# A wavelet-attention and mixture-of-experts block: the order of expert 0's last products, and expert 14 in one block

## Chip, core and metric

One Trainium2 chip, one core. The metric is device time in microseconds, the median of several runs of one kernel; a profile is one more execution, with its own time.

## What is computed

The input is x, [2, 1024, 128]. A first layer (layer norm, two wavelet levels, linear attention on the lowest band, synthesis, layer norm, residual) gives 2048 tokens of 128 features. The second layer, where the change lies, is a mixture of 16 experts that choose their tokens:

```python
scores = sigmoid(h @ gate_w.T)                       # h: 2048 normalised tokens
cap = 256                                            # 2048 / 16 * 2
topk_score, topk_ids = top_k(scores.T, cap)          # each expert takes 256 tokens
xin = h[topk_ids]
eo = silu(xin @ gw.T + gb) * (xin @ up_w.T + up_b)   # 128 -> 512, per expert
eo = eo @ down_w.T + down_b                          # 512 -> 128
out = zeros.at[topk_ids].add(eo * topk_score)
shared = (silu(x @ sh_gate.T) * (x @ sh_up.T)) @ sh_down.T   # 128 -> 256 -> 128, all tokens
result = x + out + shared
```

All of it is in 32-bit floating point.

## The kernel before, in words

Tokens lie 128 to a partition block: 16 tiles of 128 tokens, in 4 groups of 4. The first layer, the router and the search for each expert's 256th score take the first 95 us or so. Each expert's tokens then come as two chunks of 128 rows, and four engines and the DMA queues work on the experts as a pipeline whose order is written out by hand; waits are semaphores.

- **POOL** issues indirect DMAs. `gather(e, c)` (line 538) fetches chunk c of expert e's rows from DRAM into one of 7 buffers (they lie in the tensor that the profile calls hT). `scatter(e)` (line 549) adds both weighted chunks of expert e into the output, chunk after chunk; it waits first until all scatters of the expert before have landed (for expert 0: until the four base stores have), then for each chunk's weighed rows. 12 gathers go ahead; then, after each scatter, 2 (experts 0 to 5) or 1 (experts 6 to 13) gathers follow, by the tuple `BETWEEN`.
- **TensorE (PE)** takes an expert as a block of 4 products q of 128 hidden features each. `turn_x` (line 1443) transposes the gathered rows; for each q the up and gate products (lines 1488, 1489) write one of five banks; `down(q)` (line 1457) multiplies hidden features back, two products later (`LAG = 2`), into bank 3 or 4 by turns. The turn of the next expert stands in the middle of a block (after its third product).
- **ACT** does silu on each product (line 745) and `weigh`, the scaling of an expert's finished rows by their scores (line 571, one instruction for each chunk), which releases the scatter.
- **DVE** does `hidden` (line 1122), the copy of turned rows out of PSUM (`keep_x`, line 1088), the down bias (`add_bias`, line 1104), and, in the first three experts, pieces of the table that places the last eight experts' rows (lines 1020 to 1030).
- **SP** stores the base, x1 plus the shared part, group by group (line 399); the last group's store waits for `add_shared(LAST, ...)` on DVE (line 1055).

Experts 14 and 15 (`HALVED = E - 2`) are not whole blocks but two half blocks each, one for each chunk, so that a chunk can be scattered while the other is computed:

```python
BLOCKS = [(e, WHOLE) for e in range(HALVED)] + [(e, (c,)) for e in range(HALVED, E) for c in range(CH)]
WARM_B = {HALVED + 1: 2, HALVED + 2: 2, HALVED + 3: 2}
```

A half block's turn stands at its own beginning, behind the last downs of the block before. `WARM_B` puts filler products (line 1145, their result is not used) ahead of the turns of the last three half blocks.

The shared expert's last group (`shared_down(LAST, t)`, line 1343) is computed among expert 0's products, after the second one, into bank 6; expert 0's fourth product, which uses bank 6 again, waits until DVE has added it up. Expert 0's last two downs come after expert 1's first product (q = 4), and ACT weighs expert 0's rows after its silu of that product.

## Time and profile before

| what | value |
|---|---|
| median of 3 runs | 205.61 us (205.59 to 206.11) |
| the profiled execution's own time | 205.9 us |
| its span, first to last instruction | 204.1 us |
| PE busy | 182.7 us, 90% of the span |
| PE weight loads | 157.1 us |
| DVE, ACT, POOL busy | 130.3, 94.2, 127.3 us |
| mean granted TensorE clock | 0.986 of 2.4 GHz |
| scatters on POOL | 32 of 1.58 us, landing 3.3 us after the issue |
| gathers on POOL | 32 of 0.98 us, landing 2.6 us after the issue (median) |

The page lists engines by busy share, but a busy engine need not set the end. The views used here are the timeline (instructions of an engine in order of time, with the idle time before each and what ended it), the chain of work that ended last, the answers on one line's DMAs, and busy time by stretches. In a timeline row, "x4" merges four passes; a 32-bit product takes two passes. The time on a row of PE contains the drain of its last pass, so the next row's start, not the sum, tells when the array was free.

### The profile page before, as it was taken

To read this page: it belongs to the slowest core of one execution; us is meant where nothing else is said; L and a number is where in the kernel's file an instruction comes from. 1 tells how busy PE (TensorE), PEld (TensorE's weight loads), DVE (VectorE), ACT (ScalarE), POOL (GpSimd) and SP (SyncE) were. 2 spreads that over 40 slices of the span, in tenths; PEclk is the share of its full clock that TensorE was granted. 3 is DMA by queue.
4 is the path that set the end of the run, shared out by engine and by line. 5 is a ranking of instruction groups with operands and counts; after the bars stand their busy time and mean duration, and the time that the engine had idled before them with its cause. 6 is when DMAs were issued, how large, how long until landed. Compare 5 with 4: busy or idle time off the path is not lost.

```text
span 204.1 us, 3777 instructions
## 1 busy us (share of the span) xinstructions
PE 182.7 (90%) x1246; PEld 157.1 (77%) x1246; DVE 130.3 (64%) x452; ACT 94.2 (46%) x248; POOL 127.3 (62%) x195
## 2 busy tenths in 40 slices
PE   6989889999979999998999999999999979888830
PEld 6957679998936577845998999999999968777720
DVE  4888999999778787887566745544554443434420
ACT  2566612468697768120244244444444442444410
POOL 7598006455117475647766887888877778777550
PEclk9999999999999999999999999999999999999995
DMA  5799999700030271203413322432332233333311
GB/s 173 252 413 419 410 420 412 302 0 3 0 117 0 94 231 51 67 18 109 114 39 51 33 43 42 57 43 35 52 38 33 38 43 40 40 40 39 33 13 13
DMA packets 11652, 22.30 MB, mean 109 GB/s; under 512 B 1504, under 2 KB 8800, under 8 KB 11504
## 3 DMA queue, kind: packets, MB, share of 16 engines
q1 hardware_dynamic: 5968, 17.52, 22.6%
q0 software_dynamic: 5664, 4.53, 16.1%
q8 instruction: 10, 0.16, 0.3%
q14 instruction: 10, 0.08, 0.1%
HBM read 17.72 MB, written 4.33 MB: 108 GB/s over the span
## 4 chain that ended last, share of the span: by engine, by line
PE 38%; POOL 16%; DMA 14%; DVE 12%; issue 10%; ACT 5%; POOLq 1%; SPq 0%; DVEq 0%; ACTq 0%
DMA out_dram<-area,rows 13%; POOL out_dram L549 11%; PE bank L1190 7%; PE bank L1488 4%; PE bank L1331 4%; PE bank L1489 4%; POOL hT L538 3%; PE bank L1457 3%; PE bank L1145 3%; PE bank L1343 2%; POOL rstd L454 2%; DMA x_tok<-in_x_dram 2%; PE bank L1401 1%; PE bank L1293 1%; DVE junk L964 1%
## 5 line engine op out<-in xcount | busy, mean ns | idle before, releaser
L549 POOL DMA_INDIRECT out_dram<-area,rows x32 | 50.6, 1581 | 17.8 <-DMA out_dram<-area,rows 7.2
L1122 DVE SCALAR_TENSOR_TENSOR area<-bank,consts,sgate 128x256 f32<-128x256 f32 (+1 forms) x72 | 32.7, 454 | 44.8 <-ACT sgate L745 44.0
L745 ACT ACTIVATE sgate<-bank,consts 128x256 f32<-128x256 f32 (+1 forms) x72 | 32.4, 450 | 54.8 <-PE bank L1489 54.0
L1488 PE MATMUL bank<-area,wT 128*128 128x256 f32 (+1 forms) x144 | 40.4, 363 | 2.6 <-issue 2.5
L1457 PEld LDWEIGHTS bank<-wT,area 128*128 128x128 f32 x256 | 37.9, 191 | 6.0 <-DVE area L1122 2.7
L1457 PE MATMUL bank<-wT,area 128*128 128x128 f32 x256 | 40.2, 278 | 1.8 <-DVE area L1122 1.8
L538 POOL DMA_INDIRECT hT<-h_rows,rows x32 | 31.7, 991 | 13.3 <-issue 9.2
L1489 PE MATMUL bank<-area,wT 128*128 128x256 f32 (+1 forms) x144 | 39.5, 356 | 0.0
L1489 PEld LDWEIGHTS bank<-area,wT 128*128 128x128 f32 x144 | 26.1, 190 | 2.9
L1488 PEld LDWEIGHTS bank<-area,wT 128*128 128x128 f32 x144 | 21.9, 191 | 4.0 <-issue 3.8
L525 POOL TENSOR_TENSOR sh_hid<-sh_up,sgate 128x64 f32<-128x64 f32 x48 | 13.6, 322 | 15.0 <-ACT sh_up L695 12.4
L1145 PE MATMUL bank<-ident 128*128 128x128 f32 x132 | 19.9, 308 | 1.6 <-POOL ident L418 1.6
L1145 PEld LDWEIGHTS bank<-ident 128*128 128x128 f32 x132 | 18.4, 220 | 1.6 <-POOL ident L418 1.6
L1190 PE MATMUL bank<-sh_hid,area 128*128 128x128 f32 x160 | 18.6, 276 | 0.0
L1190 PEld LDWEIGHTS bank<-sh_hid,area 128*128 128x128 f32 x160 | 18.2, 192 | 0.3 <-ACT area L618 0.3
L1331 PE MATMUL bank<-hT,sh_wT 128*128 128x512 f32 x32 | 17.6, 636 | 0.6 <-ACT hT L659 0.6
L571 ACT ACTIVATE area<-area,hT 128x128 f32<-128x128 f32 x32 | 11.2, 392 | 7.9 <-DVE area L1104 7.9
L964 DVE TENSOR_SCALAR_CACHE_REDUCE junk<-area,search 128x256 bf16<-128x256 f32 (+1 forms) x30 | 13.2, 477 | 1.3 <-ACT area L673 0.8
L1343 PEld LDWEIGHTS bank<-sh_wT,sh_hid 128*128 128x128 f32 x64 | 8.5, 191 | 4.1 <-issue 2.9
L454 POOL TENSOR_TENSOR rstd<-var_eps,half_pow 128x4 f32<-128x4 f32 (+1 forms) x6 | 7.4, 1230 | 6.1 <-DVE var_eps L775 6.1
L498 POOL TENSOR_TENSOR x_tok<-x_tok,consts 128x128 f32<-128x128 f32 x4 | 3.1, 814 | 12.4 <-DVE area L887 12.4
L687 ACT ACTIVATE below<-area,search 128x256 bf16<-128x256 f32 (+1 forms) x15 | 7.6, 509 | 4.8 <-DVE search L978 4.0
(197 smaller groups left out, 265.5 us busy)
## 6 DMA issues: line engine op xcount, KB each, us to landing
wT<-in_weights_dram SPq DMA_DIRECT2D x16, 768.0 KB, 16.5
h_rows<-hrow SPq DMA_DIRECT2D x2, 576.0 KB, 3.7
x_tok<-in_x_dram SPq DMA_DIRECT2D x4, 256.0 KB, 3.6
x_tok<-in_down_b_dram SPq DMA_DIRECT2D x1, 1024.0 KB, 6.4
out_dram<-x SPq DMA_DIRECT2D x4, 256.0 KB, 2.2
hT<-h_rows,rows POOLq DMA_INDIRECT x32, 2.6
out_dram<-area,rows POOLq DMA_INDIRECT x32, 3.3
sh_wT<-in_shared_dram SPq DMA_DIRECT2D x1, 384.0 KB, 3.0
```

Source lines behind the costliest of these rows:

```text
L525: last = pool.tensor_tensor(sh_hid[:, n % 2, t, k:k + 64], sh_up[:, t, k:k + 64], sgate[:, t, k:k + 64], ALU.mult)
L538: pool.indirect_dma_start(out=gath[:, e % GBUF, c, :], out_offset=None, in_=h_rows[:, :], in_offset=bass.IndirectOffsetOnAxis(ap=rows[:, c ...
L549: pool.indirect_dma_start(out=out_rows, in_=eo[:, e % EOB, c, :], in_offset=None, out_offset=bass.IndirectOffsetOnAxis(ap=rows[:, c, e:e + ...
L745: act.activation(sgate_e[:, q % SGB, 0:n], up_bank(q)[:, CAP:CAP + n], ACT.Silu, bias=biasT[:, 1, j, e:e + 1]).then_inc(s_sil, 1)
L964: last = dve.tensor_scalar(junk[:, k, :], keys, cand[:, k:k + 1], 0.0, ALU.is_ge, ALU.add, accum_out=cnt[:, k:k + 1])
L1122: dve.scalar_tensor_tensor(hidden[:, b % 2, j, 0:n], up_bank(q)[:, 0:n], biasT[:, 0, j, e:e + 1], sgate_e[:, q % SGB, 0:n], ALU.add, ALU.m ...
L1145: pe.matmul(spare[:, 0:P], ident[:, :], ident[:, :], start=True, stop=True)
L1190: last = pe.matmul(dst, band[:, b, m0 + o:m0 + o + P], diag_c[:, d0 - 4 + k, :], start=False, stop=(d0 == 4 and o == 2), skip_group_check= ...
L1331: pe.matmul(bank[2 * kind + t][:, :], sh_wT[:, 2 * kind + t, :], rhs, start=True, stop=True).then_inc((s_shg, s_shu)[kind], 1)
L1457: last = pe.matmul(bank[3 + b % 2][:, i * P:(i + 1) * P], hidden[:, b % 2, j, i * P:(i + 1) * P], wT[:, e, 2, j, :], start=(j == 0 and i = ...
L1488: pe.matmul(up_bank(q)[:, 0:n], wT[:, e, 0, j, :], xselT[:, b % 2, 0:n], start=True, stop=True)
L1489: pe.matmul(up_bank(q)[:, CAP:CAP + n], wT[:, e, 1, j, :], xselT[:, b % 2, 0:n], start=True, stop=True).then_inc(s_gu, 1)
```

## The change

- `HALVED` becomes E - 1: expert 14 is one whole block; only expert 15 is two half blocks. A new constant `TURN_LATE = E - 2` keeps expert 14's turn, bias and weighing where a half block has them: at its own beginning. `WARM_B` becomes 5 fillers ahead of expert 14's turn and none elsewhere.
- The last group's shared products move from after expert 0's second product to after its fourth, behind `down(1)`, and from bank 6 to bank 4; they wait until DVE has read bank 4's previous content. Expert 0's last two downs follow them directly, before expert 1's first product. Expert 1's first down, which writes bank 4, waits until DVE has added the shared part.
- DVE adds the last shared part and expert 0's bias after expert 0's fourth hidden product; ACT weighs expert 0 after its fourth silu.

The diff, whole but for context lines:

```diff
     EOB = 4
-    HALVED = E - 2
+    HALVED = E - 1
+    TURN_LATE = E - 2
     LOW = 16
...
         BLOCKS = [(e, WHOLE) for e in range(HALVED)] + [(e, (c,)) for e in range(HALVED, E) for c in range(CH)]
-        WARM_B = {HALVED + 1: 2, HALVED + 2: 2, HALVED + 3: 2}
+        WARM_B = {TURN_LATE: 5}
         ODD_BANK = (bank[5], bank[4])
...
                 n = len(chunks) * P
-                if b >= HALVED and j == 0:
+                if b >= TURN_LATE and j == 0:
                     weigh(act, b - 1)
...
                                bias=biasT[:, 1, j, e:e + 1]).then_inc(s_sil, 1)
-                if q == FT or j == 2 and 1 < b < HALVED:
+                if q == FT - 1:
+                    weigh(act, 0)
+                elif j == 2 and 1 < b < TURN_LATE:
                     weigh(act, b - 1)
...
                     slot_rows(2)
-                if q == 2:
-                    add_shared(LAST, bank[6])
-                if b >= HALVED and j == 0:
+                if b >= TURN_LATE and j == 0:
                     add_bias(b - 1)
...
                                          sgate_e[:, q % SGB, 0:n], ALU.add, ALU.mult).then_inc(s_hid, 1)
-                if q == FT or j == 1 and 1 < b < HALVED:
+                if q == FT - 1:
+                    add_shared(LAST, bank[4])
+                    add_bias(0)
+                elif j == 1 and 1 < b < TURN_LATE:
                     add_bias(b - 1)
...
                     slot_rows(LATE)
-                if j == 2 and b + 1 < HALVED:
+                if j == 2 and b + 1 < TURN_LATE:
                     keep_x(b + 1)
...
                     pe.wait_ge(s_lasthid, SHT)
+                    pe.wait_ge(s_lastbase, 1)
                 if 0 < n < LAST:
...
                 for k in range(SHT):
-                    last = pe.matmul(bank[6 if n == LAST else 4][:, t * P:(t + 1) * P], sh_hid[:, n % 2, k, t * P:(t + 1) * P], sh_wT[:, 4 + k, :],
+                    last = pe.matmul(bank[4][:, t * P:(t + 1) * P], sh_hid[:, n % 2, k, t * P:(t + 1) * P], sh_wT[:, 4 + k, :],
                                      start=(k == 0), stop=(k == SHT - 1))
...
                 n = len(chunks) * P
-                if b >= HALVED and j == 0:
+                if b >= TURN_LATE and j == 0:
                     down(q - LAG)
...
                 if q == 2:
-                    for t in range(4):
-                        shared_down(LAST, t)
-                if q == 3:
-                    pe.wait_ge(s_lastbase, 2)
+                    pe.wait_ge(s_lasthid, SHT)
                 if q == 4:
...
                           stop=True).then_inc(s_gu, 1)
-                if q == FT:
+                if q == FT - 1:
                     down(q - LAG)
+                    for t in range(4):
+                        shared_down(LAST, t)
                     down(q - 1)
-                elif q >= LAG and q != FT + 1 and not (b >= HALVED and j < LAG):
+                    down(q)
+                elif q >= LAG and not ((b == 1 or b >= TURN_LATE) and j < LAG):
+                    if q == FT + LAG:
+                        pe.wait_ge(s_lastbase, 2)
                     down(q - LAG)
...
                     spread(LATE)
-                if j == 2 and b + 1 < HALVED:
+                if j == 2 and b + 1 < TURN_LATE:
                     turn_x(b + 1)
...
```

TensorE at the start of the experts, from the gate product of expert 0's second step on, first as it was (line 1343 the shared products, 1488 and 1489 up and gate products, 1457 downs, 1443 a turn):

```order
L1489 MATMUL bank1<-area,wT 128x256
L1343 MATMUL bank6<-sh_wT,sh_hid 128x128 x8
L1488 MATMUL bank2<-area,wT 128x256
L1489 MATMUL bank2<-area,wT 128x256
L1457 MATMUL bank3<-wT,area 128x128 x2
L1443 MATMUL bank5<-ident,hT 128x128 x2
L1488 MATMUL bank6<-area,wT 128x256
L1489 MATMUL bank6<-area,wT 128x256
L1457 MATMUL bank3<-wT,area 128x128 x2
L1488 MATMUL bank7<-area,wT 128x256
L1489 MATMUL bank7<-area,wT 128x256
L1457 MATMUL bank3<-wT,area 128x128 x4
```

and as it is now (1348 the shared products, 1490 and 1491 up and gate, 1462 downs, 1448 a turn):

```order
L1491 MATMUL bank1<-area,wT 128x256
L1490 MATMUL bank2<-area,wT 128x256
L1491 MATMUL bank2<-area,wT 128x256
L1462 MATMUL bank3<-wT,area 128x128 x2
L1448 MATMUL bank5<-ident,hT 128x128 x2
L1490 MATMUL bank6<-area,wT 128x256
L1491 MATMUL bank6<-area,wT 128x256
L1462 MATMUL bank3<-wT,area 128x128 x2
L1348 MATMUL bank4<-sh_wT,sh_hid 128x128 x8
L1462 MATMUL bank3<-wT,area 128x128 x4
L1490 MATMUL bank7<-area,wT 128x256
L1491 MATMUL bank7<-area,wT 128x256
```

The eight shared products have moved from ahead of expert 0's third product (bank 2) to behind its second down, and the four products of its last two downs from behind expert 1's first product (bank 7) to ahead of it.

DVE at the same place, first as it was, from expert 0's second hidden product on (line 1122 hidden products, 1055 the sum of the shared part, 1088 a copy of turned rows, 1104 a bias, 1020 a piece of the late table):

```order
L1122 SCALAR_TENSOR_TENSOR area<-bank1,consts,sgate 128x256
L1055 TENSOR_TENSOR x1<-bank6,x1 128x512
L1122 SCALAR_TENSOR_TENSOR area<-bank2,consts,sgate 128x256
L1020 TENSOR_TENSOR area<-area,digit1 128x512
L1088 COPY area<-bank5 128x256
L1122 SCALAR_TENSOR_TENSOR area<-bank6,consts,sgate 128x256
L1020 TENSOR_TENSOR area<-area,digit1 128x512
L1122 SCALAR_TENSOR_TENSOR area<-bank7,consts,sgate 128x256
L1104 TENSOR_TENSOR area<-bank3,x_tok 128x256
L1020 TENSOR_TENSOR area<-area,digit1 128x512
L1122 SCALAR_TENSOR_TENSOR area<-bank0,consts,sgate 128x256
```

and as it is now (1123, 1058, 1091, 1107 and 1023 in that order):

```order
L1123 SCALAR_TENSOR_TENSOR area<-bank1,consts,sgate 128x256
L1123 SCALAR_TENSOR_TENSOR area<-bank2,consts,sgate 128x256
L1023 TENSOR_TENSOR area<-area,digit1 128x512
L1091 COPY area<-bank5 128x256
L1123 SCALAR_TENSOR_TENSOR area<-bank6,consts,sgate 128x256
L1058 TENSOR_TENSOR x1<-bank4,x1 128x512
L1107 TENSOR_TENSOR area<-bank3,x_tok 128x256
L1023 TENSOR_TENSOR area<-area,digit1 128x512
L1123 SCALAR_TENSOR_TENSOR area<-bank7,consts,sgate 128x256
L1023 TENSOR_TENSOR area<-area,digit1 128x512
```

The sum of the shared part stands behind the fourth hidden product (bank 6) instead of the second, with expert 0's bias directly behind it, ahead of expert 1's first hidden product (bank 7) instead of behind it.

TensorE at the end, from expert 13's last downs on, first as it was, to the end of the first half block of expert 14:

```order
L1457 MATMUL bank4<-wT,area 128x128 x6
L1443 MATMUL bank5<-ident,hT 128x128
L1488 MATMUL bank1<-area,wT 128x128
L1489 MATMUL bank1<-area,wT 128x128
L1488 MATMUL bank2<-area,wT 128x128
L1489 MATMUL bank2<-area,wT 128x128
L1488 MATMUL bank6<-area,wT 128x128
L1489 MATMUL bank6<-area,wT 128x128
L1457 MATMUL bank3<-wT,area 128x128
L1488 MATMUL bank7<-area,wT 128x128
L1489 MATMUL bank7<-area,wT 128x128
L1457 MATMUL bank3<-wT,area 128x128 x3
```

and as it is now, behind the same downs of expert 13, to the end of the whole block of expert 14 (1149 are fillers):

```order
L1149 MATMUL bank1<-ident 128x128 x5
L1448 MATMUL bank5<-ident,hT 128x128 x2
L1490 MATMUL bank1<-area,wT 128x256
L1491 MATMUL bank1<-area,wT 128x256
L1490 MATMUL bank2<-area,wT 128x256
L1491 MATMUL bank2<-area,wT 128x256
L1490 MATMUL bank6<-area,wT 128x256
L1491 MATMUL bank6<-area,wT 128x256
L1462 MATMUL bank3<-wT,area 128x128 x2
L1490 MATMUL bank7<-area,wT 128x256
L1491 MATMUL bank7<-area,wT 128x256
L1462 MATMUL bank3<-wT,area 128x128 x6
```

One block with products of 256 columns, its turn behind five fillers, stands in the place of two half blocks; behind it the two half blocks of expert 15 follow without fillers.

## Rows read from the trace of the kernel before

**Rows 1.** Timeline of POOL at the end: start us, us, line, operation, [idle before, releaser].

```profile
175.61 1.02 POOL L538 DMA_INDIRECT hT<-h_rows,rows  x1 [0.30 <-issue]
...
186.62 1.02 POOL L538 DMA_INDIRECT hT<-h_rows,rows  x1 [0.30 <-issue]
...
193.68 1.55 POOL L549 DMA_INDIRECT out_dram<-area,rows  x1 [1.97 <-DMA out_dram<-area,rows]
196.96 1.55 POOL L549 DMA_INDIRECT out_dram<-area,rows  x1 [1.73 <-ACT area L571]
```

**Rows 2.** Timeline of POOL, scatters of experts 0, 1 and 2.

```profile
105.34 1.62 POOL L549 DMA_INDIRECT out_dram<-area,rows  x1 [1.49 <-ACT area L571]
...
112.66 1.61 POOL L549 DMA_INDIRECT out_dram<-area,rows  x1 [1.23 <-ACT area L571]
...
119.13 1.61 POOL L549 DMA_INDIRECT out_dram<-area,rows  x1 [0.35 <-issue]
```

**Rows 3.** Timeline of PE at the start of the experts.

```profile
96.78 1.95 PE L1343 MATMUL bank<-sh_wT,sh_hid 128*128 128x128 f32 x16
...
106.60 0.61 PE L1457 MATMUL bank<-wT,area 128*128 128x128 f32 x4
107.34 0.67 PE L1488 MATMUL bank<-area,wT 128*128 128x256 f32 x2
```

**Rows 4.** Timeline of PE, expert 13's turn and first product.

```profile
168.69 0.44 PE L1443 MATMUL bank<-ident,hT 128*128 128x128 f32 x2 [1.37 <-DMA hT<-h_rows,rows]
168.97 0.60 PE L1488 MATMUL bank<-area,wT 128*128 128x256 f32 x2
...
169.83 0.61 PE L1457 MATMUL bank<-wT,area 128*128 128x128 f32 x4
```

**Rows 5.** Timeline of PE, end of expert 13 and the half blocks.

```profile
175.07 1.05 PE L1457 MATMUL bank<-wT,area 128*128 128x128 f32 x8
176.32 0.71 PE L1457 MATMUL bank<-wT,area 128*128 128x128 f32 x4 [0.19 <-DVE area L1122]
176.87 0.27 PE L1443 MATMUL bank<-ident,hT 128*128 128x128 f32 x1
177.79 0.46 PE L1488 MATMUL bank<-area,wT 128*128 128x128 f32 x2 [0.65 <-issue]
...
181.10 0.49 PE L1457 MATMUL bank<-wT,area 128*128 128x128 f32 x2 [0.40 <-DVE area L1122]
181.42 0.61 PE L1145 MATMUL bank<-ident 128*128 128x128 f32 x4
181.87 0.27 PE L1443 MATMUL bank<-ident,hT 128*128 128x128 f32 x1
182.57 0.46 PE L1488 MATMUL bank<-area,wT 128*128 128x128 f32 x2 [0.43 <-issue]
...
195.43 0.49 PE L1457 MATMUL bank<-wT,area 128*128 128x128 f32 x2 [0.40 <-DVE area L1122]
```

**Rows 6.** Timeline of DVE, the copy of expert 2's rows.

```profile
106.82 0.42 DVE L1088 COPY area<-bank 128x256 f32<-128x256 f32 x1
```

**Rows 7.** Base stores: the queue's issues (last start at the end), and the page's landing.

```profile
L399 SPq DMA_DIRECT2D out_dram<-x x4: 372/375/378, 76.4 to 99.5; - x4
...
out_dram<-x SPq DMA_DIRECT2D x4, 256.0 KB, 2.2
```

**Rows 8.** Landing of single gathers, issued at 175.61 and at 186.62 us.

```profile
DMA to landing us min/median/max: 2.6/2.6/2.6
...
DMA to landing us min/median/max: 4.5/4.5/4.5
```

**Rows 9.** DMA queues from 189.0 to 189.2 us: packets, MB, share of 16 engines.

```profile
q8 instruction: 1, 0.02, 31.6%
```

**Rows 10.** Stretches: us, busy of PE, PEld, DVE, ACT, POOL, granted clock, DMA, GB/s.

```profile
180.00:185.00 5.00, 4.17 (x34) 3.63 (x33) 2.14 (x7) 1.87 (x5) 3.66 (x4) 1.00 0.26 33
...
198.00:199.00 1.00, 0.00 (x0) 0.00 (x0) 0.00 (x0) 0.00 (x0) 0.51 (x1) 0.65 0.00 0
```

## The prediction

> **What bounds the kernel now.** Start at the end, with POOL's timeline. The last scatter is issued at 196.96 us, and POOL had stood idle 1.73 us in front of it, released by ACT [rows 1]; the span ends at 204.1 us, so 7.1 us of landing and closing follow that issue whatever releases it. The scatter before it, at 193.68 us, waited for something else: the landing of the previous expert's scatter. So two chains meet there. One is POOL's: scatter, scatter, gather, wait for the landing, again. The other is TensorE's tail, which delivers expert 15's second half. At the very end TensorE's is the later one, by 196.96 - (193.68 + 1.55 + 0.30) = 1.43 us, where 1.55 us is one scatter on POOL and 0.30 us the step between two issues [rows 1].
>
> Then follow POOL's chain back. From expert 2's scatter at 119.13 us on it waits only for its own issue (0.35 us there) and for its own transfers, but expert 1's, at 112.66 us, waited 1.23 us for ACT [rows 2]. So the chain is as early as expert 1's weighed rows are, and these follow TensorE, which computes without a gap except for short ones: 0.29 us, for instance, in front of expert 2's first product (the down before it starts at 106.60 us and takes the array 0.45 us, four passes, so it could start at 107.05; it starts at 107.34) [rows 3, 5].
>
> **The start: expert 0's last down products and the shared ones.** TensorE executes the same instructions; only their order changes, so the work is at price zero and what counts is the waits. The shared products (16 passes from 96.78 us [rows 3]) now come after two more products of expert 0, a turn and two downs, about 2 x 0.86 + 0.28 + 2 x 0.45 = 2.9 us later [rows 4, 5]. They now cover the latency from expert 0's last product to its last down, which is 1.25 us elsewhere (175.07 to 176.32 [rows 5]). What was late before: the copy of expert 2's rows on DVE stood at 106.82 us, and the product needing it at 107.34 [rows 3, 6]. It stood there because ACT took expert 0's weighing one product later and the activations behind it were pushed into each other; now weighing stands one product earlier, with a copy at some 106.4 us by the same durations. I take the stall as gone: 0.29 us. The other ends: 0 if TensorE waits as long elsewhere, and 0.93 us if expert 1's rows come so early that POOL itself is the limit (its 1.23 us of idle less the usual 0.30 [rows 2]). I take 0.29 because it is the only gap that this order plainly removes.
>
> What is late next: the last base store. It follows the shared products through DVE and SP, so it is issued near 99.5 + 2.9 = 102.4 us and lands 2.2 us later, at 104.6 us [rows 7]. Expert 0's scatter waits for it and started at 105.34 us [rows 2]; there is 0.7 us of cover. Should it run late by more, expert 0's scatter slips but expert 1's only beyond that 0.93 us. On DVE, the shared sum (behind expert 0's fourth hidden product now) makes DVE wait for TensorE, with expert 0's bias and one piece of the table behind it; the next hidden product is needed only after two whole products of TensorE, so I cost it at nothing.
>
> **The tail: expert 14 whole and turned late.** Before, the last 4 half blocks take 182.57 - 177.79 = 4.78 us each [rows 5]. Now there is one whole block and two halves, and 5 fillers instead of 6 in all, all of them ahead of expert 14. In order, everything 0.29 us earlier:
> - Expert 13's last downs leave TensorE free at 176.87 - 0.29 = 176.58 us [rows 5]. Five fillers at 0.45 / 2 us each (two took 181.87 - 181.42 us [rows 5]) end at 177.71 us.
> - The turn of expert 14 now needs both chunks. The second one's gather is issued at 175.61 - 0.29 us [rows 1] and took 2.6 us [rows 8]: 177.92 us. So the fillers lie inside that wait and cost nothing; the wait itself costs 1.3 us against the old start.
> - Turn to first product: 177.79 - 176.87 = 0.92 us for a half [rows 5]; for two chunks I take 1.0. Four products at 0.86 us [rows 4] with one down (0.45 us) between them: 178.92 + 3.89 = 182.81 us. Last down 1.25 us later, next turn 0.55 us after that (176.32 to 176.87): 184.61 us [rows 5].
> - Half block: 0.92 us to its first product, 181.10 - 177.79 = 3.31 us to its last down, 0.32 us to the next turn (181.10 to 181.42) [rows 5]: 189.16 us. Expert 15's second gather, issued at 186.62 - 0.29 us, has landed at 188.93 us if it takes 2.6 us.
> - Second half: 189.16 + 0.92 + 3.31 = 193.39 us for the last down, and 196.96 - 195.43 = 1.53 us through DVE and ACT to POOL [rows 1, 5]: expert 15's second half is ready at 194.92 us, 2.0 us before the old 196.96.
>
> **The sum.** POOL's chain, 0.29 us earlier, issues the last but one scatter at 193.39 us and can issue the last at 193.39 + 1.55 + 0.30 = 195.24 us. That is later than 194.92, so POOL is the bound now and 0.3 us of TensorE's gain is lost on it. The last issue moves from 196.96 to 195.24 us: 1.72 us. The profiled execution took 205.9 us (span 204.1), so it would be 204.2; the median of the runs is 0.3 us below that execution, 205.61, which gives 203.9 us. Bounds of the unknown start: 0 gives 195.53 us for the last issue and 204.2; 0.93 gives 203.2.
>
> **A rule on gathers, weighed.** Expert 15's second gather took 4.5 us instead of 2.6 [rows 8], and while it was in flight, at 189.0 us, an instruction packet of 0.02 MB went over the same 16 DMA engines [rows 9]. So landing is not one number, and this change makes two landings count that had slack.
> The Trainium skill (DMA: Bandwidth & Descriptors, "Why a DMA increments its semaphore by 16 and not by 1") says that a DMA issued by GpSimd is complete only when all 16 engines have reported. By that rule one busy engine delays the whole gather, and the sum would be the first rival's; the two rows agree with it.
>
> **Rivals.**
> *A gather lands late.* If expert 15's second one again takes 4.5 us, it lands at 190.83 us; then 0.70 us to the product (181.87 to 182.57, no bias ahead of the copy) [rows 5], 3.31 and 1.53: ready at 196.37 us, 0.6 us better than before, 205.0 us. If expert 14's second chunk takes 4.5 us, everything behind it is 1.9 us later: 196.82 us, 205.5. For it: the old 4.5 us belongs to just this gather. Against it: the tail has fewer instructions, so the packet may come after the landing. It decides beyond 0.3 us of delay.
> *The start gives nothing.* POOL's chain then stays where it was, and the last issue is at 195.53 us: 204.2 us. For it: expert 1's rows pass through ACT and DVE, whose order I filled in by estimate.
> *The clock falls in the tail.* Slower. The granted clock is 1.00 in the tail with two fillers at each of three boundaries [rows 10]; without them each of two boundaries leaves some 0.9 us without a product, after a wait for a gather. At half the clock a half block's 16 passes of products, 2 of the last down and 1 of the turn, 0.11 us each [rows 5], grow by 2.1 us. If it falls before the first half block, both grow: ready at 194.92 + 4.2 = 199.1 us, 2.2 us later than before, 207.8 us. If it falls only for the last one, the time is 197.0 us and nothing changes; so it decides from the first half block on. Against it: the clock was still granted full after the last down of 195.43 us and fell only in the stretch from 198 to 199 us, to 0.65 on average [rows 5, 10], and no wait in the new tail is as long as that one.
> The Trainium skill (TensorE: Matmul & The Clock Gate, "What's actually happening") says "the default state is throttled, and activity releases the throttle". By that rule dropping fillers speaks against this change and would give this rival's time; no row of this trace shows it fall between blocks.
>
> **How the numbers follow.** Forecast 0.50; start gives nothing 0.20; late gather 0.24; clock 0.06. A measurement of this kernel can tell about 0.3%, 0.6 us. The first two are faster; a late gather is at the edge, so half of it is faster and half the same: faster 0.82, same 0.12, slower 0.06. The range reaches from the 0.93 us bound of the start, 203.2, to just past expert 15's late gather, 205.2; outside stay the clock and a late gather of expert 14.
>
> **What would show it.** Right: no stall in front of expert 2's first product; expert 1's scatter near 112.4 us; TensorE waiting for a gather in front of expert 14's turn until about 177.9 us; the last down near 193.4 us; POOL's last scatter released by "issue", not by ACT, near 195.2 us; clock 1.00 until then. Wrong: the last scatter still released by ACT (a late gather, or a longer tail than I added up), expert 1's scatter not earlier, or a granted clock below 1 before the last down.

## The result, and the profile after

| | time, us (runs) | ratio to before |
|---|---|---|
| before | 205.81 median, 205.46 to 208.13 (20) | |
| the change | 204.62 median, 203.94 to 207.02 (20) | 0.9922, 95% interval 0.9899 to 0.9945 |
| predicted | 203.9, range 203.2 to 205.2 | |

It is 1.2 us faster, inside the range and 0.7 us above the number. Nine of its 20 executions lie from 203.94 to 204.28 us, where the sum put them; the profiled one took 206.19 us (span 204.4) and is one of the worst. That is luck for a reader: it shows two of the three rivals at once, and what they cost can be read off. Some executions of most kernels here, of before too, took about 1.5 us more, and where the profile of one was such an execution (run 10 below) it shows TensorE's clock at half for 3 us at 50 us, long before the change's place.

First POOL's timeline of the changed kernel (start, length, line, operation, idle before it and its releaser; line 539 is a gather, 550 a scatter), at the start of the experts and at the end:

```profile
105.04 1.62 POOL L550 DMA_INDIRECT out_dram<-area,rows  x1 [1.14 <-DMA out_dram<-x]
...
112.23 1.61 POOL L550 DMA_INDIRECT out_dram<-area,rows  x1 [1.09 <-ACT area L572]
...
186.09 1.01 POOL L539 DMA_INDIRECT hT<-h_rows,rows  x1 [0.30 <-ACT area L572]
...
189.68 1.55 POOL L550 DMA_INDIRECT out_dram<-area,rows  x1 [0.30 <-issue]
193.28 1.55 POOL L550 DMA_INDIRECT out_dram<-area,rows  x1 [2.04 <-DMA out_dram<-area,rows]
197.28 1.55 POOL L550 DMA_INDIRECT out_dram<-area,rows  x1 [2.44 <-ACT area L572]
```

Expert 1's scatter stands at 112.23 us (112.66 before [rows 2]), the last but one at 193.28 us (193.68 [rows 1]; 193.39 predicted). The last one stands at 197.28 us, later than the old 196.96, and ACT releases it, not POOL. In every profile of this case the time of the execution is the issue of the last scatter plus 8.9 to 9.0 us (196.96 and 205.9 before, 197.28 and 206.19 here), so this one row tells the whole time.

TensorE's timeline in the same execution (1149 fillers, 1448 turns, 1490 the up products, 1462 downs):

```profile
176.27 1.28 PE L1149 MATMUL bank<-ident 128*128 128x128 f32 x10
177.82 0.44 PE L1448 MATMUL bank<-ident,hT 128*128 128x128 f32 x2 [0.27 <-DMA hT<-h_rows,rows]
178.82 0.67 PE L1490 MATMUL bank<-area,wT 128*128 128x256 f32 x2 [0.56 <-issue]
...
184.04 0.71 PE L1462 MATMUL bank<-wT,area 128*128 128x128 f32 x4 [0.19 <-DVE area L1123]
184.59 0.27 PE L1448 MATMUL bank<-ident,hT 128*128 128x128 f32 x1
185.52 0.46 PE L1490 MATMUL bank<-area,wT 128*128 128x128 f32 x2 [0.65 <-issue]
...
188.82 0.49 PE L1462 MATMUL bank<-wT,area 128*128 128x128 f32 x2 [0.40 <-DVE area L1123]
190.45 0.33 PE L1448 MATMUL bank<-ident,hT 128*128 128x128 f32 x1 [1.14 <-DMA hT<-h_rows,rows]
191.21 0.77 PE L1490 MATMUL bank<-area,wT 128*128 128x128 f32 x2 [0.43 <-issue]
...
195.75 0.49 PE L1462 MATMUL bank<-wT,area 128*128 128x128 f32 x2 [0.30 <-DVE area L1123]
```

Down to 188.82 us this is the predicted tail almost to the hundredth. Then the turn waits 1.14 us for a gather, and the last half block takes 195.75 - 191.21 = 4.54 us from its first product to its last down instead of 3.31 [rows 5]. Two more views say why. The landing of the gather issued at 186.09 us:

```profile
DMA to landing us min/median/max: 4.3/4.3/4.3
```

and an instruction packet on the DMA queues in the tenth of a microsecond from 188.3 us (packets, MB, share of 16 engines):

```profile
q8 instruction: 1, 0.02, 60.7%
```

The busy time by stretches (us, then PE, PEld, DVE, ACT, POOL, the granted clock, DMA share, GB/s) shows the clock:

```profile
188.00:189.00 1.00, 0.60 (x5) 0.41 (x5) 0.35 (x1) 0.37 (x1) 1.00 (x1) 1.00 0.12 35
189.00:190.00 1.00, 0.31 (x2) 0.12 (x2) 0.29 (x1) 0.33 (x1) 0.69 (x2) 1.00 0.08 4
190.00:191.00 1.00, 0.33 (x1) 0.14 (x1) 0.18 (x1) 0.07 (x1) 1.00 (x1) 0.92 0.64 62
191.00:192.00 1.00, 0.79 (x4) 0.82 (x5) 0.11 (x1) 0.00 (x0) 0.24 (x1) 0.50 0.26 10
192.00:193.00 1.00, 1.00 (x6) 1.00 (x6) 0.16 (x1) 0.37 (x1) 0.00 (x0) 0.50 0.48 56
```

The clock went from full (2.4 GHz) to half (1.2 GHz) near 190.9 us, after three microseconds in which TensorE was busy for 0.60, 0.31 and 0.33 us. By rows: with the gather alone the last scatter would stand at 190.45 + 0.70 + 3.31 + 1.53 = 195.99 us; the clock adds the other 1.3. It is at full again before the half block ends (0.88 granted from 194 to 195 us, 1.00 in the next).

### The profile page after: what moved, and what is told of

It is laid out like the page before. It is cut to its first block, busy times and chain, and to the rows that moved or that the text cites. A ratio compares the mean times of both kernels' runs of the same rounds, so it can differ in the third digit from the quotient of the medians.

```text
span 204.4 us, 3723 instructions
## 1 busy us (share of the span) xinstructions
PE 182.7 (89%) x1228; PEld 157.3 (77%) x1228; DVE 129.0 (63%) x446; ACT 93.0 (45%) x244; POOL 127.4 (62%) x195
## 4 chain that ended last, share of the span: by engine, by line
PE 38%; DMA 16%; POOL 14%; DVE 12%; issue 10%; ACT 5%; POOLq 1%; DVEq 0%; ACTq 0%
DMA out_dram<-area,rows 14%; POOL out_dram L550 10%; PE bank L1194 7%; PE bank L1490 4%; PE bank L1335 4%; PE bank L1491 4%; PE bank L1462 3%; PE bank L1149 3%; POOL hT L539 3%; PE bank L1348 2%; POOL rstd L455 2%; PE bank L1406 1%; PE bank L1297 1%; DMA x_tok<-in_x_dram 1%; DVE junk L967 1%
## 5 line engine op out<-in xcount | busy, mean ns | idle before, releaser
L1123 DVE SCALAR_TENSOR_TENSOR area<-bank,consts,sgate 128x256 f32<-128x256 f32 (+1 forms) x68 | 31.8, 468 | 44.5 <-ACT sgate L746 44.2
L746 ACT ACTIVATE sgate<-bank,consts 128x256 f32<-128x256 f32 (+1 forms) x68 | 31.3, 461 | 55.1 <-PE bank L1491 55.0
L1462 PE MATMUL bank<-wT,area 128*128 128x128 f32 x256 | 39.5, 278 | 1.1 <-DVE area L1123 1.1
L1149 PE MATMUL bank<-ident 128*128 128x128 f32 x130 | 19.1, 305 | 1.6 <-POOL ident L419 1.6
L1149 PEld LDWEIGHTS bank<-ident 128*128 128x128 f32 x130 | 17.7, 217 | 1.6 <-POOL ident L419 1.6
```

Source lines behind the costliest of these rows:

```text
L746: act.activation(sgate_e[:, q % SGB, 0:n], up_bank(q)[:, CAP:CAP + n], ACT.Silu, bias=biasT[:, 1, j, e:e + 1]).then_inc(s_sil, 1)
L1123: dve.scalar_tensor_tensor(hidden[:, b % 2, j, 0:n], up_bank(q)[:, 0:n], biasT[:, 0, j, e:e + 1], sgate_e[:, q % SGB, 0:n], ALU.add, ALU.m ...
L1149: pe.matmul(spare[:, 0:P], ident[:, :], ident[:, :], start=True, stop=True)
L1462: last = pe.matmul(bank[3 + b % 2][:, i * P:(i + 1) * P], hidden[:, b % 2, j, i * P:(i + 1) * P], wT[:, e, 2, j, :], start=(j == 0 and i = ...
```

## The experiments

Each time is a median with its lowest and highest and the number of runs; ratios are to runs of before on the same chip. A last scatter is read from the profiled execution's POOL timeline.

| run | time, us | ratio | last scatter, releaser |
|---|---|---|---|
| 1 start alone | 205.70 (205.24 to 207.74, 12) | 0.9979 (0.9949 to 1.0010) | 196.32 ACT |
| 2 tail alone | 205.25 (204.90 to 207.23, 12) | 0.9961 (0.9931 to 0.9990) | 196.37 issue |
| 3 two more fillers | 204.67 (204.28 to 206.16, 12) | 0.9935 (0.9904 to 0.9966) | 195.43 ACT |
| 4 gather earlier | 205.37 (205.08 to 207.28, 12) | 0.9969 (0.9936 to 1.0002) | 196.16 issue |
| 5 the change again | 204.76 (204.16 to 206.95, 12) | 0.9933 (0.9900 to 0.9966) | 195.48 issue |
| 6 no fillers | 204.92 (204.43 to 207.00, 12) | 0.9926 (0.9893 to 0.9959) | 196.73 ACT |
| 7 earlier weighing | 205.12 (204.38 to 207.10, 12) | 0.9954 (0.9924 to 0.9985) | 195.46 issue |
| 8 gather late | 210.80 (210.38 to 211.32, 4) | 1.0217 (1.0165 to 1.0268) | 201.39 ACT |
| 9 the same, filled | 209.77 (208.94 to 210.72, 4) | 1.0186 (1.0132 to 1.0240) | 200.02 ACT |
| 10 32 passes more | 206.54 (204.80 to 208.29, 12) | 0.9987 (0.9948 to 1.0025) | 197.41 ACT |
| 11 the same, earlier weighing | 205.21 (204.54 to 208.29, 12) | 0.9954 (0.9919 to 0.9990) | 195.75 issue |
| 12 30 passes, no price | 203.84 (203.65 to 205.41, 6) | 0.9893 (0.9858 to 0.9928) | 194.75 ACT |

**1 and 2: each part alone.** The change with the old tail, and the old start with the new tail (in run 2 the conditions on expert 14's turn, bias and weighing name `TURN_LATE` as in the change):

```diff
 run 1, from the change
-    HALVED = E - 1
+    HALVED = E - 2
...
-        WARM_B = {TURN_LATE: 5}
+        WARM_B = {HALVED + 1: 2, HALVED + 2: 2, HALVED + 3: 2}
```

```diff
 run 2, from before
-    HALVED = E - 2
+    HALVED = E - 1
+    TURN_LATE = E - 2
...
-        WARM_B = {HALVED + 1: 2, HALVED + 2: 2, HALVED + 3: 2}
+        WARM_B = {TURN_LATE: 5}
...
```

> Only the start is changed; experts 14 and 15 stay four half blocks with two fillers at three boundaries. Theory (two chains; before, TensorE's tail is the later one, and it is released by gathers of POOL's chain, so it moves with expert 1's scatter): expert 1's scatter near 112.2 us instead of 112.66, the last scatter still released by ACT, near 196.5 us, the time 0.4 us shorter (ratio 0.998). Rival 1 (the start gives nothing, all of the gain is the tail's): no change, expert 1's scatter at 112.6 us. Rival 2 (the start carries the gain): 1.2 us or more.

> Only the tail is changed; shared products and expert 0's downs stand where they were. Theory: POOL's chain stays where it was, the last but one scatter near 193.7 us, the last at 195.5 us where expert 15's second gather lands within 2.6 us: 1.4 us shorter (ratio 0.993). Where that gather lands late (4.3 us or so), the last scatter is released by ACT at 196.5 us or later, and the clock may have fallen before the last half block. Rival (the tail's gain hangs on the earlier start): less than 0.7 us even in runs without a late gather.

The start alone gains 206.06 - 205.70 = 0.36 us, the tail alone 0.81 us; together 1.17, near what the change gains (1.19). So the medians add up, though the interval of each ratio is some 0.6 us wide to either side. The tail alone had been priced at more. Its profile shows TensorE where it should be, with the last down at 193.86 us, but POOL's chain late by itself:

```profile
194.51 1.55 POOL L550 DMA_INDIRECT out_dram<-area,rows  x1 [2.63 <-DMA out_dram<-area,rows]
196.37 1.55 POOL L550 DMA_INDIRECT out_dram<-area,rows  x1 [0.30 <-issue]
```

The scatter of 190.33 us landed some 3.9 us after its issue (worked out from the wait behind it) instead of 3.3, with an instruction packet on q8 at 191.7 us, so that wait was 2.63 us where it is 1.94 in run 3. Once POOL is the bound, a late scatter costs its whole delay. This one execution is not all of the miss: 195.5 us for the last scatter would have made a time of 204.4, and the fastest of the twelve took 204.90. Why is not shown.

In run 1's profile a scatter was later still:

```profile
194.11 1.55 POOL L550 DMA_INDIRECT out_dram<-area,rows  x1 [2.76 <-DMA out_dram<-area,rows]
```

The scatter before it, of 189.80 us, took 4.0 us to land, and no q8 packet came in its flight: the nearest had come at 188.0 us.

**3: two fillers ahead of the last half block.**

```diff
-        WARM_B = {TURN_LATE: 5}
+        WARM_B = {TURN_LATE: 5, HALVED + 1: 2}
```

> The change with two more fillers ahead of the last half block's turn. Theory (the change's own loss in its profiled execution is a gather that lands 1.7 us late, and on top of it 1.2 us because the clock fell to 1.2 GHz while TensorE waited for it): no cost in executions without a late gather, since the fillers replace the wait for the bias on DVE but for 0.2 us, and POOL has 0.2 us of slack there: near 204.0 us; in executions with a late gather the granted clock stays at 1.00 through the last half block (3.3 us from its first product to its last down, not 4.5), so the slowest executions come down by about 1 us. Rival (the clock falls for another reason, or fillers this few do not hold it): the same spread as the change, the last half block again 4.5 us where the gather is late.

In its profile the gather took 2.7 us, the clock stayed at 1.00, and the fillers pushed the last down to 193.90 us. The last scatter, at 195.43 us, then waited 0.48 us with ACT as its releaser: the two chains end nearly together. The median does not differ from the change's. As the gather was in time here, this run does not show what the fillers do for the clock when it is late; runs 8 and 9 do.

**4: expert 15's second gather moved ahead of two scatters.**

```diff
-    BETWEEN = (2, 2, 2, 2, 2, 2, 1, 1, 1, 1, 1, 1, 1, 1, 0, 0)
+    BETWEEN = (2, 2, 2, 2, 2, 2, 1, 1, 1, 1, 1, 1, 2, 0, 0, 0)
```

> The change with expert 15's second gather issued behind expert 12's scatters instead of expert 13's. Theory (POOL's chain sets the end where no gather is late): one more gather in that period makes it 6.3 us instead of 5.3 or 5.4, so the last two scatters are issued about 0.95 us later than in an undisturbed execution of the change, near 194.2 and 196.1 us, both with ACT's rows long ready; TensorE never waits for that gather, the clock stays at 1.00 until the last down, and the times lie close together near 205.0 us. Rival (TensorE's tail sets the end, POOL has room): no later than the change's undisturbed 204.0 us.

The gather is out of danger (issued at 182.09 us, needed at 189.35) and the last down comes at 193.45 us, but the scatters behind it are about 1 us later, 188.89 and 190.74 us instead of 187.80 and 189.68, and the last is at 196.16 us with POOL's own issue as releaser. So the POOL chain does set the end when TensorE is on time. The times had been expected close together, and are not: nine are at 205.08 to 205.69 us, three at 206.94 to 207.28, so a late gather of expert 15 is not what makes those long.

**5: the change again.**

> The change itself, unedited, beside the other kernels of this set. If expert 15's second gather lands 2.6 to 2.7 us after its issue (186.1), the turn in front of the last half block stands near 189.15, the last down near 193.4, the last scatter is released by POOL's own issue near 195.1, and the time of the profiled execution is some 204.0. If it takes 4.3 us or more, the turn stands at 190.4 or later, the last scatter is released by ACT near 196.0 with the clock at 1.00 until the last down, and near 197.3 if the clock falls once more; the time is then 204.9 or 206.2. The theory that the landing alone decides allows nothing in between but landings in between. The rival, that the changed tail is longer by itself, gives a last down behind 194.5 with a gather of 2.6 us too.

In this execution (204.48 us) expert 15's second gather, issued at 186.16 us, landed after 2.7 us. POOL at the end:

```profile
189.82 1.55 POOL L550 DMA_INDIRECT out_dram<-area,rows  x1 [0.30 <-issue]
193.63 1.55 POOL L550 DMA_INDIRECT out_dram<-area,rows  x1 [2.25 <-DMA out_dram<-area,rows]
195.48 1.55 POOL L550 DMA_INDIRECT out_dram<-area,rows  x1 [0.30 <-issue]
```

and TensorE behind it:

```profile
189.31 0.27 PE L1448 MATMUL bank<-ident,hT 128*128 128x128 f32 x1
190.10 0.46 PE L1490 MATMUL bank<-area,wT 128*128 128x128 f32 x2 [0.52 <-issue]
...
193.41 0.49 PE L1462 MATMUL bank<-wT,area 128*128 128x128 f32 x2 [0.40 <-DVE area L1123]
```

Same kernel, same code: 4.3 us of landing against 2.7, with what the wait did to the clock, made the last scatter 197.28 or 195.48 us. The rival, a tail that is longer by itself, falls. Here POOL's issue releases the last scatter, as predicted; TensorE's part would have been ready at 193.41 + 1.53 = 194.94 us (194.92 predicted).

**6: no fillers.**

```diff
-        WARM_B = {TURN_LATE: 5}
+        WARM_B = {}
```

> The five fillers ahead of expert 14's turn are left out (their result is not used). Theory of the prediction: they lie inside the wait for the gather, so the turn still stands near 177.8 and nothing moves: same time as the change, within 0.2 us, and the clock stays at 1.00, because the wait of TensorE is then 1.5 us, about what it was with fillers plus 1.1. Where the gather of expert 13's second chunk is late and the fillers end after the landing, it is 0.1 to 0.4 us faster. Rival, the clock falls without them: granted clock below 1.00 in the stretch from 177 to 185, each product of expert 14's block nearly 1.7 us instead of 0.86 for as long as it lasts, 1 to 4 us slower.

The median is the change's within the spread, but the profiled execution shows the rival. TensorE from expert 13's last down on:

```profile
176.14 0.71 PE L1462 MATMUL bank<-wT,area 128*128 128x128 f32 x4 [0.19 <-DVE area L1123]
178.10 0.44 PE L1448 MATMUL bank<-ident,hT 128*128 128x128 f32 x2 [1.25 <-DMA hT<-h_rows,rows]
179.10 0.97 PE L1490 MATMUL bank<-area,wT 128*128 128x256 f32 x2 [0.56 <-issue]
179.86 1.06 PE L1491 MATMUL bank<-area,wT 128*128 128x256 f32 x2
...
186.01 0.71 PE L1462 MATMUL bank<-wT,area 128*128 128x128 f32 x4 [0.19 <-DVE area L1123]
```

and its stretch:

```profile
178.00:185.00 7.00, 6.34 (x25) 5.22 (x26) 1.88 (x4) 1.50 (x5) 5.44 (x5) 0.76 0.30 32
```

The turn is no earlier than with fillers (178.10; 177.98 us in run 5), so they did cost nothing. But products stood 0.85 us apart instead of 0.43 for as long as the clock was at half, and the last down of expert 14 came 186.01 - 178.10 = 7.91 us after the turn, where the change takes 184.04 - 177.82 = 6.22: the clock cost 1.7 us in this execution. In the eleven profiles of the new tail with these fillers the granted clock is 1.00 from 178 to 185 us. How often it falls without them the times do not show; the fillers are a cheap insurance, no more was shown.

**7: weighing one product earlier.** Expert 1's scatter waits for ACT; here ACT weighs experts 1 and 2 after their successors' second product instead of the third, and DVE copies expert 3's rows ahead of one hidden product.

```diff
-                elif j == 2 and 1 < b < TURN_LATE:
+                elif j == (1 if b < 4 else 2) and 1 < b < TURN_LATE:
...
+                if q == 10:
+                    keep_x(3)
...
-                if j == 2 and b + 1 < TURN_LATE:
+                if j == 2 and b + 1 < TURN_LATE and b != 2:
```

> ACT weighs experts 1 and 2 one product earlier (and the copy of expert 3's rows on DVE stands a little earlier, so that ACT's order fits). Theory: expert 1's weighed rows release POOL's chain, so its scatter starts near 111.9 instead of 112.23, and everything behind it on POOL is 0.33 us earlier up to the gathers of the last experts; TensorE in the tail waits for these gathers, so the last scatter moves by the same 0.3 us: 0.3 us faster than the change. Rival: the products behind the weighing get their activation later, TensorE is stalled at experts 1 to 3 and the last scatter is bound by TensorE, so nothing or less than nothing is gained. A scatter of expert 1 at 112.2 says that the weighing was not what it waited for.

From expert 0's scatter to expert 1's it is 6.84 us (105.18 to 112.02) against 7.19 (105.04 to 112.23): the chain does start 0.35 us earlier, and expert 15's second gather is issued at 185.90 us. But the last scatter is at 195.46 us as in run 5, because the scatter of 189.47 us took 3.9 us to land, with a q8 packet at 191.3 us. A gain of 0.3 us at the head of the chain is smaller than what one late landing takes at its end; the median says nothing in its favour.

**8 and 9: what the clock costs, by itself.** Expert 15's second gather is issued only behind expert 14's scatters, so that TensorE must wait some 5 us; run 9 fills that wait.

```diff
 run 8
-    BETWEEN = (2, 2, 2, 2, 2, 2, 1, 1, 1, 1, 1, 1, 1, 1, 0, 0)
+    BETWEEN = (2, 2, 2, 2, 2, 2, 1, 1, 1, 1, 1, 1, 1, 0, 1, 0)
...
 run 9, besides
-        WARM_B = {TURN_LATE: 5}
+        WARM_B = {TURN_LATE: 5, HALVED + 1: 20}
```

> Expert 15's second gather is issued only behind expert 14's two scatters, near 191.5 instead of 186.1, so that it lands near 194.1 and TensorE waits about 5 us in front of the last half block, with no filler. Theory that a wait for a gather of this length costs the clock: granted clock near 0.5 for about 3 us behind the first product, the last down 4.5 us after the first product instead of 3.3, the last scatter near 200.9 and a time of 209.8. Rival, the clock falls in such a wait for another reason or by chance: clock 1.00, last down 3.3 us after the first product, last scatter near 199.6, time 208.5.

> The kernel with expert 15's second gather issued late (last half block's turn near 194.5, wait of TensorE 4.6 us), plus 20 fillers (0.225 us each, 4.5 us) in that wait; their result is not used. Theory: TensorE's activity in the wait is what keeps the clock. Granted clock 1.00 through the last half block, the first product 0.70 us behind the turn (195.2 instead of 195.42), the last down 3.31 us behind that (198.5 instead of 199.86), the last scatter near 200.0 instead of 201.39 and the time near 209.0 instead of 210.4. Rival, fillers don't hold it or the fall has another cause: clock 0.50 and a last down behind 199.6 again, time 210.2 or more.

TensorE's last half block without fillers, run 8:

```profile
189.38 0.49 PE L1462 MATMUL bank<-wT,area 128*128 128x128 f32 x2 [0.40 <-DVE area L1123]
194.51 0.47 PE L1448 MATMUL bank<-ident,hT 128*128 128x128 f32 x1 [4.64 <-DMA hT<-h_rows,rows]
195.42 0.77 PE L1490 MATMUL bank<-area,wT 128*128 128x128 f32 x2 [0.43 <-issue]
...
199.86 0.49 PE L1462 MATMUL bank<-wT,area 128*128 128x128 f32 x2 [0.21 <-DVE area L1123]
```

and with them, run 9:

```profile
189.42 4.63 PE L1149 MATMUL bank<-ident 128*128 128x128 f32 x40
194.43 0.33 PE L1448 MATMUL bank<-ident,hT 128*128 128x128 f32 x1 [0.38 <-DMA hT<-h_rows,rows]
195.19 0.46 PE L1490 MATMUL bank<-area,wT 128*128 128x128 f32 x2 [0.43 <-issue]
...
198.49 0.49 PE L1462 MATMUL bank<-wT,area 128*128 128x128 f32 x2 [0.39 <-DVE area L1123]
```

The turns stand 0.08 us apart, the last downs 1.37. In run 8 the granted clock is 0.71 from 191 to 192 us and 0.50 from there until 198, in run 9 1.00 throughout. The fillers in the wait are the only edit between the two, so they are what held the clock, and its fall costs a half block 4.44 - 3.30 = 1.14 us from first product to last down. That is the second loss in the profile of the change, measured alone. The times say it less clearly: two of run 9's four executions, at 210.42 and 210.72 us, are as slow as run 8's, and no profile shows why.

**10 to 12: moving the packets.** The idea is that the q8 packets come at TensorE's pace: in four profiles (before, the change, runs 5 and 8), from 89 us on, 103 to 154 recorded passes of TensorE lie between one and the next, and in run 8 the 131 passes around the long wait took 30.5 us. (Over all fourteen profiles it is 83 to 167, so the count alone is a loose guide.) If so, more passes early in TensorE's program bring the late packets forward, out of the flights that matter.

```diff
+            def tick(n, spare):
+                for _ in range(n):
+                    pe.matmul(spare[0:32, 0:32], ident[:, 0:32], ident[:, 0:32], start=True, stop=True)
+
-            stay_warm(18, bank[7])
+            stay_warm(15, bank[7])
+            tick(10, bank[7])
...
-            WARM_I, WARM_S, WARM_L, WARM_C = 2, 6, 3, 4
+            WARM_I, WARM_S, WARM_L, WARM_C = 2, 5, 3, 4
...
                     stay_warm(WARM_S, bank[6 + n % 2])
+                    tick(4, bank[6 + n % 2])
```

Run 11 adds the edits of run 7. Run 12 has 14 for 15, `WARM_S` 4 for 5 and `tick(5, ...)`: 30 passes more, with less time in them.

> The change, with 32 more passes in TensorE's program far ahead of the experts: 3 of 18 wide fillers before the first layer become 10 narrow ones (32x32), and in three places of the search one of 6 wide fillers becomes 4 narrow ones; no result is used, the time of the wide ones taken out is about that of the narrow ones put in. Theory: the instruction packets on q8 are TensorE's own, fetched as its program advances (about 130 passes from one to the next in the runs so far, 22 us or, with a wait of 4.6 us, 30 us), so the packets near 166 and near 188 to 191 move to near 161 and near 183 to 185, and no gather that TensorE waits for is then in flight: expert 13's second gather, which took 3.4 to 4.6 us in every run so far, takes 2.6 to 2.7, and expert 15's second takes 2.6 to 2.7. The last scatter is then released by POOL's own issue near 195.1 every time and the time is 204.0, with a median lower than the change's by some 0.5. Rival, the packets come by the clock on the wall or of another engine: packets at 166 and 188 to 191 again, expert 13's gather late again, same time as the change.

> The same 32 passes, and ACT weighing experts 1 and 2 one product earlier as in the run before of that kind. Theory: with the gathers of experts 13 and 15 landing in time, POOL's chain is the bound to the end, and it starts 0.3 us earlier (expert 1's scatter some 0.35 us earlier against expert 0's), so the last scatter is near 194.8 and the time 203.7, 0.3 us less than with the shift alone. Rival: TensorE's tail, which waits for gathers and then adds 17 us of work, is the later one and the 0.3 us are lost: same time as with the shift alone, last scatter released by ACT.

> The shift again, this time without its price at the front: 4 of 18 wide fillers before the first layer become 10 narrow ones, and in three places of the search two of 6 wide fillers become 5 narrow ones, 30 passes more in all. Theory: the price of the run before (0.9 us at the first scatter) was that of narrow fillers that outlasted their wait, so expert 0's scatter is back near 105.1; the packets on q8 again come 5 to 6 us earlier than in the change (near 160 and 183), the gathers of experts 13 (second chunk) and 15 (second chunk) take 2.6 to 2.7, and from expert 0's scatter to the last one it takes 89.9 us as in the two runs before: last scatter near 195.0, released by POOL's own issue, time of a run without another disturbance 203.9, median some 204.3, below the change's 204.7. Rival: the packets jitter by more than the shift, so that one of the two gathers is late again and the time is the change's, 204.7.

Run 10's time was spoiled ahead of the experts: its first scatter stands at 107.56 us (105.01 in run 5), 1.6 us of it by TensorE's clock at half near 50 us and 0.9 by narrow fillers that outlasted their waits; run 11, without the former, has it at 105.94. So their times say nothing for the shift. From the first scatter to the last, however, it is 89.85 us in run 10 and 89.81 in run 11 against 90.47 in run 5, and expert 13's second gather, 3.4 to 4.6 us in every profile until then, took 2.6 in both. The packets now fell into other flights: expert 15's first gather took 4.0 us in run 10 and 3.6 in run 11, expert 13's first 3.5 in run 10. The second gathers of both experts, which had been the ones to hold TensorE up, were in time. The earlier weighing added nothing again. Run 12 took the front's price away (first scatter 105.14 us) and is the fastest kernel here. POOL at its end:

```profile
189.39 1.55 POOL L550 DMA_INDIRECT out_dram<-area,rows  x1 [0.30 <-issue]
192.89 1.55 POOL L550 DMA_INDIRECT out_dram<-area,rows  x1 [1.94 <-DMA out_dram<-area,rows]
194.75 1.55 POOL L550 DMA_INDIRECT out_dram<-area,rows  x1 [0.30 <-ACT area L572]
```

and the landing of its gather of 185.89 us:

```profile
DMA to landing us min/median/max: 2.5/2.5/2.5
```

Five of its six executions lie from 203.65 to 203.91 us. Its ratio, 0.9893, overlaps with the change's interval, and the two were not run side by side, so that it beats before is shown and that it beats the change is likely. Nor is all of its gain the packets': by the scatter of 187.51 us (187.94 in run 5) its chain is already 0.43 us ahead, gained little by little since 155.25 us, where both stand together, and why is not shown. The expectation held for the last packet (181.9 us, where it was 188.0 to 191.7 in the profiles of before, the change and runs 1 to 5) and failed for the one near 166: it stood at 166.0 us, and expert 13's gather took 4.0 us again. The packet of 181.9 us fell into the flight of expert 15's first gather (3.7 us), which had time to spare. The shift is seen for the one, not for the other.

## Why the prediction was right, and what it missed

**The bound.** Two chains meeting at the last scatter, POOL's and TensorE's tail: right. Runs 2, 4, 5, 7 and 11 end on POOL's issue, the change's profile and run 6 on TensorE's tail, runs 3, 10 and 12 on both almost together.

**The start.** Its size was right, its place only partly. Expert 2's first product in the change and the row before it:

```profile
101.24 1.06 PE L1462 MATMUL bank<-wT,area 128*128 128x128 f32 x8
102.13 0.60 PE L1490 MATMUL bank<-area,wT 128*128 128x256 f32 x2
...
106.25 0.61 PE L1462 MATMUL bank<-wT,area 128*128 128x128 f32 x4
106.90 0.67 PE L1490 MATMUL bank<-area,wT 128*128 128x256 f32 x2
```

It is 0.44 us earlier than 107.34 [rows 3]. Of these, 0.16 are no merit of the change: expert 0's first product, on code that nobody touched, already stood at 94.10 us against this row of before:

```profile
94.26 0.67 PE L1488 MATMUL bank<-area,wT 128*128 128x256 f32 x2 [0.56 <-issue]
```

That leaves 0.28 us, and 0.29 was predicted. But the step "I take the stall as gone" failed: the copy came at 106.38 us as forecast (106.4), and yet 106.90 - (106.25 + 0.45) = 0.20 us of the 0.29 remain. The rest came from a gap that the prediction had not looked at. Before, expert 1's second product followed the down that now stands elsewhere:

```profile
100.96 0.61 PE L1457 MATMUL bank<-wT,area 128*128 128x128 f32 x4
101.52 0.67 PE L1488 MATMUL bank<-area,wT 128*128 128x256 f32 x2
```

101.52 - (100.96 + 0.45) = 0.11 us; no such gap is left there. The remaining 0.08 is spread over sixteen rows, each rounded. Against the rival "the start gives nothing" speaks run 1, with 0.36 us; the interval of its ratio, 0.9949 to 1.0010, would not exclude nothing. The profiles do it better: expert 1's scatter stands at 112.21 to 112.40 us in the nine that have the new start and neither the earlier weighing nor the shift's delay, and at 112.51 (run 2) and 112.66 us (before) in the two with the old one.

The base store was issued at 102.2 us (102.4 predicted) but landed after 2.6 us, not 2.2 [rows 7], and so released expert 0's scatter, at 105.04 us. The 0.7 us of cover were gone, and nothing was lost, since expert 1's scatter still waited 1.09 us for ACT: the bound that the prediction put behind it.

**The tail, in its steps.** Fillers inside the wait for expert 14's gather: right (0.27 us of wait were left behind them). Turn 177.82 (177.92 predicted), first product 178.82 (178.92), last down 184.04 (184.06), next turn 184.59 (184.61), half block 185.52 (185.53) to 188.82 (188.84). Durations from rows of expert 13's whole block and of the half blocks carried over without a correction. Where the gather landed in time, the rest held too: 193.41 us for the last down (193.39), with POOL's last issue at 195.48 (195.24, the difference being one scatter that landed 0.2 us later).

**The late gather**, held at 0.24, happened in the profiled execution, as it was described: 4.3 us, a packet of instructions in flight. In the fourteen profiles (before, the change, twelve runs) 19 gathers issued after 158 us took 3.4 to 4.6 us, and each had a q8 packet in its flight; of the others whose landing is recorded only one had (run 3, a packet just as it landed), and none took over 2.7 us. The Trainium skill (DMA: Bandwidth & Descriptors, "Why a DMA increments its semaphore by 16 and not by 1") has a DMA of GpSimd complete only when all 16 engines have reported; these landings agree. They do not prove it: no row shows a single engine, the packet of the view above took 0.607 x 16 x 0.1 = 0.97 us of engine time where the gather lost 1.7, and earlier a packet often did no harm (gathers of 130 us in runs 3, 4 and 9 had one in their flight and took 2.6 or 2.7 us). What the prediction missed is that scatters land late too (runs 1, 2 and 7, 3.9 to 4.0 us instead of 3.3), which matters as soon as POOL is the bound. Whether the packet does that is not shown: in runs 2 and 7 one was in flight, in run 1 none, and run 4's scatter of 190.74 us had one at 191.3 and was not late (2.01 us of wait behind it).

**The clock** is where a step failed: "no wait in the new tail is as long as that one". It was argued from the waits of an undisturbed tail, and the two rivals were given separate chances; but a late gather makes just such a wait, and the clock fell in it: with the turn at 190.45 us, the last scatter stood at 197.28 us instead of 195.99. So a late gather was priced at 205.0 as a median, 205.3 for a single execution, and cost 206.19 us in one where it brings the clock with it. The sum for it stood there ("if it falls only for the last one"), only not added to the other. Its size was too large: 2.1 us for a half block at half clock, where 4.54 - 3.31 = 1.23 us were measured here and 1.14 in run 8, since the clock was at full again before the block ended. The Trainium skill (TensorE: Matmul & The Clock Gate, "What's actually happening") says that activity releases the throttle; runs 6, 8 and 9 agree (0.76 from 178 to 185 us without fillers; 0.50 without and 1.00 with them in the long wait), the fall at 50 us in run 10 does not fit it, since TensorE was computing at the time.

**The number.** 203.9 us is near the lowest of the times (203.94; nine are at 204.28 or below), the median is 204.62. Of the 0.7 us between, 0.2 lies in the reference: its 205.61 us was a median of three runs, and over twenty it is 205.81, so most of the 0.3 us by which the sum went from the profiled execution to the median was chance. Late landings of gathers and scatters in part of the executions may make up the rest; with one profile for each set of times that is not shown. Nor do the runs show that 0.24 for a late gather was too low: of the six profiles with the new tail, its order of gathers and no shift (the change, runs 2, 3, 5, 6 and 7), expert 15's second gather was late in one.

## What to carry to other kernels

When a change makes two chains end together, price the late landing of every DMA that then counts, gathers and scatters alike, and price it with what the wait behind it does to TensorE's clock: the two are one case, not two. Fillers ahead of a wait for a gather cost nothing here where they ended before the landing, and where the clock fell without them they were worth 1.7 us (run 6) and 1.4 us (run 8). Read several profiles of one kernel before explaining a time by one of them: here 1.7 us lay between the profiled executions of the same code (206.19 and 204.48).

## What the runs showed of the hardware that was not expected

- The packets on q8 move with TensorE's program. Runs 10 and 12 differ from the change in TensorE's instructions alone, and the packet that stands at 88.9 to 89.3 us in the eleven profiles without the shift came at 84.2 to 84.5 us in runs 10 to 12. Run 8 fits: 131 recorded passes lie between two packets around its long wait and took 30.5 us, where the intervals in the other three of the four profiles counted are 14 to 25 us. With 30 or 32 passes more ahead of the experts the last one came at 181.8 to 182.2 us (with the front's delay of runs 10 and 11 taken off here and above) instead of 188.0 or later. Its place scatters by several microseconds between executions of one kernel (188.3 and 191.1 us for the change), and the packet near 166 us moved in runs 10 and 11 and not in run 12. What decides that was not found.
- The clock can fall while TensorE computes. In run 10, from 49 us on (columns as above):

```profile
49.00:50.00 1.00, 1.00 (x10) 1.00 (x10) 0.97 (x4) 1.00 (x4) 1.00 (x2) 1.00 0.00 0
50.00:51.00 1.00, 1.00 (x8) 1.00 (x7) 0.93 (x5) 0.53 (x2) 0.08 (x1) 0.64 0.07 16
51.00:52.00 1.00, 1.00 (x7) 1.00 (x6) 0.93 (x9) 0.00 (x0) 0.00 (x0) 0.50 0.00 0
```

It was busy all of this time, and had been before: all of the six microseconds from 42 us and 0.65 of the one from 48 us. The fourteen passes of fillers took 2.62 us instead of 1.81 (run 5). Run 5, without the fall, was as busy there (7.65 of the 8 us from 42 us, all of the four behind). The cause stays open.
